# Two steps of value products in a row, six places for probabilities, and one weight loaded in each pass

## The chip, the core and the metric

The kernel is written for one NeuronCore of a Trainium2 chip. The core has five engines with queues of their own: TensorE (matrix products, its weight loads shown as PEld), VectorE (DVE), ScalarE (ACT), GpSimd (POOL) and SyncE (SP, which here only issues DMAs). They meet at semaphores alone. The metric is the device time of one execution in microseconds.

## What is computed

The reference runs a decoder of two layers over 4 sequences of 1024 rows of 256, with a context of 154 rows for each:

```python
x = x + attn0(layernorm(x))              # 16 heads of 16, causal, keys and values mixed with a gated memory
x = x + xattn0(layernorm(x), ctx, ctx)   # 16 heads, rotary, keys from the context
x = x + ffn0(layernorm(x))               # quantised linear, depthwise convolution, silu
x = x + attn1(layernorm(x))              # 16 heads of 16, every row sees every row
x = x + xattn1(layernorm(x), ctx, ctx)   # one head of 256 over the context
x = x + moe(layernorm(x))                # 16 experts, 2 chosen, and a shared one

def heads(q, k, v):                      # the part that the change is about
    w = softmax(einsum('bqd,bkd->bqk', q, k) / 4.0, axis=-1)
    return einsum('bqk,bkd->bqd', w, v)
```

## The kernel before

The program is written out by hand: every engine has its own list, and waits on semaphores whose counts a first dry build works out. One pass over the program handles one sequence, so there are four passes. In a pass there are three attentions of 16 heads: "own" (causal, 8 tiles of 128 keys), "cross" (two tiles of keys, 128 and 26) and "second" (8 tiles of keys, not causal). They are called the first, the cross and the third attention in this document, and all run through the same class `Heads`, with one order of work from `attention_plan`. All engines walk through this one list, each doing its own part of an item. Heads are handled in pairs, eight pairs to an attention.

The items of the list:
- *first* (a unit `u` of a head `h`): TensorE multiplies queries by keys into one of three banks (4, 5 and 6, taken in turn by `ring`; L646, up to 512 columns; causal units add a mask, L652 or L649). VectorE takes the maximum of each row (L796, into `tops`). These maxima are needed before the real scores. In the third attention a pair has 32 units.
- *join* and *cut*: VectorE joins the maxima (L803), and GpSimd cuts each into three bf16 parts (L846 to L849).
- *top*: TensorE turns the parts (L725, a bank of the ring), ScalarE copies them (L769), and SP writes them by DMA (L909) as three more rows under the queries of the pair.
- *score* (a step `s` of 128 keys, and one of its parts): TensorE computes the scores again, turned, with the maxima subtracted by those three rows (L674), for both heads of the pair, into one of two pairs of banks (0 and 1, 2 and 3). ScalarE takes the exponential (L756) and writes it into a place of `probs`. There are four places, used in turn. In the first attention GpSimd clears the masked half for pairs 1 to 5 (L837); for the others TensorE adds a mask (L678).
- *value*: TensorE multiplies values by the probabilities (L708) into bank 7, and sums over the steps. A product has 32 output rows and takes one of four strips of the array: heads times parity of the tile. The operands are f32, so each of the four is two instructions, eight for a step.
- *gather*, *spin* and *norm*, after the last step of a pair: ScalarE copies bank 7 (L763), TensorE turns it (L717, a bank of the ring), VectorE divides by the sum (L812, L814).
- *turn*, once per four pairs: the output is turned for the projection (L731).

`attention_plan` sets how these mix. Scores and values make the main list. A step of scores has one or two parts, and a step's values come as soon as the steps after it have two parts:

```python
            held.append((pair, s))
            while sum(len(steps[later]) for _, later in held[1:]) >= 2:
                value(*held.pop(0))
```

The first scores run ahead of that list by a lead, and are dealt out evenly between its entries (`upto`): per pair of the third attention 32 units over 24 entries. SP loads the queries and keys of pair + 3 (L863, L869) once the last scores of a pair are in. ScalarE's exponential `n` waits for the values that read the place four before it.

Weights of the last attention (`xattn1`) stay in memory for the whole program, among them `wide_q`, 128 x 512 words; it is used once per pass, near the end of the third attention (L1685).

## Time and profile before

| | us |
|---|---|
| median of three runs | 3350.33 |
| lowest and highest of them | 3348.94, 3357.76 |
| the profiled execution | 3356.7 |
| its span, from first to last instruction | 3355.1 |

The profile shows one execution. Each engine has a busy time; a matmul's record lasts longer than the time until the next can follow, so two matmuls overlap in the records, and distances between starts tell more than durations. A line of the timeline merges like instructions in a row: start, time from the first start to the last end, engine, line of the kernel, operation, what is written and read, shapes, and their count; in brackets the idle time of the engine ahead of it and what ended that. The page's last part lists DMA issues with the median time from issue to landing.

### The profile page before, as it was taken

How to read it: one execution, taken by the hardware profiler on the slowest of the kernel's cores; microseconds unless marked ns; L12 is line 12 of the kernel's file. 1: busy time of each engine (PE TensorE's matmuls, PEld its weight loads, DVE VectorE, ACT ScalarE, POOL GpSimd, SP SyncE). 2: the span in 40 equal slices, each digit the busy share in tenths (PEclk: the TensorE clock that was granted, in tenths of full speed). 3: DMA queues.
4: the chain of work that ended last, by engine and by line, in shares of the span. 5: the costliest groups of instructions: out<-in, count | busy, mean ns of one | idle time of the engine just before them, and what ended most of it. 6: DMA issues, size and time to landing. Idle time of an engine off the chain costs nothing.

```text
span 3355.1 us, 46975 instructions
## 1 busy us (share of the span) xinstructions
PE 3191.1 (95%) x17720; PEld 1713.3 (51%) x17720; DVE 2323.0 (69%) x4331; ACT 1782.8 (53%) x2551; POOL 634.7 (19%) x1166
## 2 busy tenths in 40 slices
PE   6999889999999989999999998999999999899999
PEld 4444433378644443337864444334786444433477
DVE  7856688556685578856678557885667855788555
ACT  3565546643456555664355555566424655556632
POOL 0322010024132201012403120100340321020033
PEclk9999999999999999999999999999999999999999
DMA  3212011023121202111312020120231202021023
GB/s 138 51 34 39 1 34 34 11 65 114 32 52 26 40 1 38 30 35 53 115 38 43 18 40 1 39 39 25 63 105 42 40 17 39 5 44 30 10 84 96
DMA packets 118101, 147.74 MB, mean 44 GB/s; under 512 B 25384, under 2 KB 75920, under 8 KB 117596
## 3 DMA queue, kind: packets, MB, share of 16 engines
q1 hardware_dynamic: 117876, 144.74, 18.1%
q8 instruction: 141, 2.31, 0.3%
q14 instruction: 84, 0.69, 0.1%
HBM read 74.25 MB, written 4.46 MB: 23 GB/s over the span
## 4 chain that ended last, share of the span: by engine, by line
PE 51%; DVE 8%; ACT 4%; issue 2%; DMA 1%; SPq 1%; POOL 0%; DVEq 0%; ACTq 0%
PE psum L1908 13%; PE psum L708 9%; PE psum L674 8%; PE psum L646 7%; PE psum L1000 4%; DVE small L796 3%; ACT work L756 2%; PE psum L939 1%; PE psum L717 1%; PE psum L500 1%; DMA work<-work 1%; PE psum L481 1%; PE psum L929 1%; SPq L863 1%; PE psum L1734 1%
## 5 line engine op out<-in xcount | busy, mean ns | idle before, releaser
L796 DVE TENSOR_REDUCE small<-psum 128x1 f32<-128x512 f32 (+6 forms) x1856 | 1136.7, 656 | 210.2 <-PE psum L646 175.9
L756 ACT ACTIVATE work<-psum 128x1024 f32<-128x1024 f32 (+5 forms) x1024 | 918.3, 935 | 419.4 <-PE psum L674 317.4
L646 PE MATMUL psum<-work 96*128 96x512 bf16 (+4 forms) x2688 | 655.7, 308 | 32.8 <-DVE small L796 16.2
L1908 PE MATMUL psum<-rounded_work 128*128 128x512 f32 x2592 | 602.0, 394 | 9.9 <-DVE rounded_work L1994 6.5
L674 PE MATMUL psum<-work 99*128 99x512 bf16 (+4 forms) x2048 | 564.2, 358 | 6.9 <-ACT work L756 4.0
L1908 PEld LDWEIGHTS psum<-rounded_work 128*128 128x128 f32 x2592 | 489.9, 190 | 116.0 <-DVE rounded_work L1994 8.3
L708 PE MATMUL psum<-work 128*32 128x512 f32 (+4 forms) x4480 | 532.3, 528 | 1.6 <-ACT work L756 1.4
L646 PEld LDWEIGHTS psum<-work 96*128 96x128 bf16 x2688 | 233.5, 97 | 544.4 <-DVE small L796 332.2
L674 PEld LDWEIGHTS psum<-work 99*128 99x128 bf16 (+1 forms) x2048 | 178.5, 97 | 199.3 <-ACT work L756 63.1
L2009 ACT CAST rounded_work<-work 128x512 fp32r<-128x512 f32 x144 | 89.4, 621 | 344.5 <-DVE work L2050 321.7
L846 POOL CAST small<-small 128x16 bf16<-128x16 f32 x96 | 18.8, 196 | 1156.2 <-DVE small L803 586.8
L1438 PE MATMUL psum<-ident_bf 128*128 128x512 bf16 x808 | 201.3, 380 | 8.7 <-DVE work L1539 4.5
L812 DVE RECIPROCAL small<-psum 128x16 f32<-128x16 f32 x96 | 24.7, 257 | 243.1 <-PE psum L717 243.1
L2055 DVE TENSOR_TENSOR rounded_work<-work,rounded_work 128x512 fp32r<-128x512 f32 x144 | 118.4, 822 | 107.2 <-ACT rounded_work L2009 107.2
L1885 POOL CAST rounded_work<-work 128x256 fp32r<-128x256 f32 x192 | 100.3, 523 | 435.9 <-PE psum L1908 421.8
L708 PEld LDWEIGHTS psum<-work 128*32 128x32 f32 (+1 forms) x4480 | 94.0, 107 | 171.4 <-issue 143.9
L2045 DVE TENSOR_TENSOR work<-work,psum 128x512 f32<-128x512 f32 x144 | 98.7, 685 | 99.5 <-PE psum L1908 89.4
L1886 POOL TENSOR_TENSOR rounded_work<-work,rounded_work 128x256 fp32r<-128x256 f32 x192 | 148.1, 772 | 15.4
L1438 PEld LDWEIGHTS psum<-ident_bf 128*128 128x128 bf16 x808 | 77.8, 98 | 93.1 <-DVE work L1539 7.8
L2050 DVE TENSOR_TENSOR work<-work 128x512 f32<-128x512 f32 x128 | 114.2, 892 | 14.7 <-DMA work<-combine 10.4
L1000 PE MATMUL psum<-xT,qkv 128*128 128x512 f32 x256 | 113.1, 593 | 2.7 <-ACT xT L488 2.7
L1000 PE MATMUL psum<-xT,work 128*128 128x512 f32 x256 | 110.5, 592 | 0.0
(297 smaller groups left out, 3765.2 us busy)
## 6 DMA issues: line engine op xcount, KB each, us to landing
work<-work SPq DMA_DIRECT2D x320, 192.0 KB, 4.3
work<-combine SPq DMA_DIRECT2D x64, 512.0 KB, 4.1
work<-in_w_gate SPq DMA_DIRECT2D x64, 128.0 KB, 3.5
work<-in_w_up SPq DMA_DIRECT2D x64, 128.0 KB, 3.5
work<-in_w_down SPq DMA_DIRECT2D x64, 128.0 KB, 3.8
work<-in_x SPq DMA_DIRECT2D x8, 512.0 KB, 4.9
out<-x SPq DMA_DIRECT2D x8, 512.0 KB, 2.9
work<-work SPq DMA_DIRECT2D x64, 28.9 KB, 2.0
```

Source lines behind the costliest of these rows:

```text
L646: ins = nc.tensor.matmul(dst[:, c * n:(c + 1) * n], A.q_pair[0:ROWS, slot, h, P * i:P * (i + 1)], A.k_of(pair, h)[0:ROWS, s0:s0 + n], star ...
L674: ins = nc.tensor.matmul(dst[0:size, 0:P * many].rearrange("p (i c) -> p i c", c=P), A.k_of(pair, h)[0:MORE_ROWS, P * s:P * s + size], til ...
L708: ins = nc.tensor.matmul(dst, V_head, moving, start=(s == 0), stop=(s == A.ns - 1), skip_group_check=True)
L756: nc.scalar.activation(probs[0:size, n % 4, :, 0:P * many], banks(2 * (n % 2), 2)[0:size, :, 0:P * many], ACT.Exp, scale=DH ** -0.5).then_ ...
L796: nc.vector.tensor_reduce(tops[:, pair % 2, places[0]:places[-1] + 1:step], src, AX.X, ALU.max) \
L1000: ins = nc.tensor.matmul(out, w[:, a, P * k:P * (k + 1)], xT[:, a, 1 + HALF * half:1 + HALF * (half + 1)], start=(a == 0), stop=(a == KD - 1))
L1438: nc.tensor.matmul(bank(place).rearrange("p (a c) -> p a c", c=P), ident_bf[:, :], spread(ident_bf[:, :], 1, 4), start=True, stop=True, sk ...
L1885: pool_own(nc.gpsimd.tensor_copy(shape(hi_w), source))
L1886: ins = nc.gpsimd.tensor_tensor(shape(lo_w), source, shape(hi_w.bitcast(F32)), ALU.subtract)
L1908: ins = nc.tensor.matmul(dst, a_parts[i], b_parts[j], start=start and n == 0, stop=stop and n == 2, skip_group_check=True)
L2050: nc.vector.tensor_tensor(value, value, row[e % 2][:, HALF * half:HALF * (half + 1)], ALU.mult).then_inc(*up("unit_full", u))
L2055: nc.vector.tensor_tensor(hid_low[:, u % 4, :], value, hid_high[:, u % 4, :].bitcast(F32), ALU.subtract).then_inc(*up("unit_ready", u))
```

## The change

The values of two steps are multiplied one behind the other, once the steps after the two have two parts. So the entries of the main list are fewer (20 in place of 24 per pair of the third attention), and the first scores are dealt out over them. `probs` has six places. `wide_q` leaves the weights that stay; SP loads it into the work area in each pass, behind the *top* of pair 6 of the third attention and ahead of that pair's rows, after the heads in the loaded slots have landed, and TensorE waits for it ahead of its use. In the changed file lines after the planner stand 4 to 10 lower.

```diff
+PROBS = 6
...
-    def value(pair, s):
-        pieces = [("value", pair, s)]
-        if s == len(steps) - 1:
+    def values(pair, s):
+
+        pieces = [("value", pair, s), ("value", pair, s + 1)]
+        if s + 1 == len(steps) - 1:
             pieces.append(("gather", pair))
...
             held.append((pair, s))
-            while sum(len(steps[later]) for _, later in held[1:]) >= 2:
-                value(*held.pop(0))
-    for which in held:
-        value(*which)
+            while sum(len(steps[later]) for _, later in held[2:]) >= 2:
+                values(*held[0])
+                held = held[2:]
+    for which in held[::2]:
+        values(*which)
...
-        probs = area.take(4, 2, HALF)
+        probs = area.take(PROBS, 2, HALF)
...
+        wide_q = area.take(KD, D)
...
-                    if n >= 4:
-                        act.wait_ge(*at("valued", a, *A.order[n - 4][0:2]))
+                    if n >= PROBS:
+                        act.wait_ge(*at("valued", a, *A.order[n - PROBS][0:2]))
...
                         sp.wait_ge(*at("scored", a, A.last_of(pair - A.slots, A.ns - 1)))
+                    if a == "second" and pair == PAIRS_OF_HEADS - 2:
+                        for loaded in range(PAIRS_OF_HEADS - SLOTS, PAIRS_OF_HEADS):
+                            for h in range(2):
+                                sp.wait_ge(*at(LOADED[2 * (loaded % SLOTS) + h], a, loaded))
+                        nc.sync.dma_start(wide_q, io["wide_q"]).then_inc(*up("context_keys_landed", "wide_q", by=16))
...
                 if n == 2:
+                    pe.wait_ge(*at("context_keys_landed", "wide_q"))
                     for a in range(KD):
-                        ins = project(dst[:, S * a:S * (a + 1)], lambda k: resident["wide_q"][:, k, P * a:P * (a + 1)], wide_kT)
+                        ins = project(dst[:, S * a:S * (a + 1)], lambda k: wide_q[:, k, P * a:P * (a + 1)], wide_kT)
```

Where the instructions stand, in three places. In the middle of a pair of the third attention TensorE's list before is this (L646 first scores, L674 scores, L708 values):

```order
L646 MATMUL psum<-work 128x512 x2
L674 MATMUL psum<-work 128x512 x2
L646 MATMUL psum<-work 128x512
L708 MATMUL psum<-work 32x512 x4
L646 MATMUL psum<-work 128x512
L674 MATMUL psum<-work 128x512 x2
L646 MATMUL psum<-work 128x512 x2
```

and now, with the same three as L650, L678 and L712:

```order
L650 MATMUL psum<-work 128x512 x2
L678 MATMUL psum<-work 128x512 x2
L650 MATMUL psum<-work 128x512
L678 MATMUL psum<-work 128x512 x2
L650 MATMUL psum<-work 128x512 x2
L678 MATMUL psum<-work 128x512 x2
L650 MATMUL psum<-work 128x512 x2
L678 MATMUL psum<-work 128x512 x2
L650 MATMUL psum<-work 128x512
L712 MATMUL psum<-work 32x512 x8
```

Values come once for four score pairs and eight units, not once for two and four.

At the top transpose of the third attention (L725, now L729) TensorE's list is, before, with the semaphores that each waits for:

```order
L725 MATMUL psum<-ident_bf,small 48x128 [waits largest,top_cut]
L674 MATMUL psum<-work 128x512 [waits prob]
L674 MATMUL psum<-work 128x512
L646 MATMUL psum<-work 128x512 [waits largest] x2
L674 MATMUL psum<-work 128x512 [waits prob]
L674 MATMUL psum<-work 128x512
L646 MATMUL psum<-work 128x512 [waits top_turned]
L708 MATMUL psum<-work 32x512 x4
L646 MATMUL psum<-work 128x512 [waits largest]
L674 MATMUL psum<-work 128x512 [waits prob,top_rows_landed_1]
```

and now:

```order
L729 MATMUL psum<-ident_bf,small 48x128 [waits largest,top_cut]
L650 MATMUL psum<-work 128x512 [waits largest]
L678 MATMUL psum<-work 128x512 [waits prob]
L678 MATMUL psum<-work 128x512
L650 MATMUL psum<-work 128x512 [waits largest]
L678 MATMUL psum<-work 128x512 [waits prob]
L678 MATMUL psum<-work 128x512
L650 MATMUL psum<-work 128x512 [waits top_turned]
L650 MATMUL psum<-work 128x512 [waits largest]
L678 MATMUL psum<-work 128x512 [waits prob,top_rows_landed_1]
```

The scores that wait for the landed rows still come third after the transpose, with no values ahead of them.

On SP, near the end of the third attention, the list now is (L867 and L873 load keys and queries, L918 writes the rows of a top, L917 the weight):

```order
L867 DMA work<-work 96x1x1024 x2
L873 DMA work<-work 96x1x1024 x2
L917 DMA work<-in_wide_q 128x512
L918 DMA work<-work 3x16x128 x2
```

The new transfer stands ahead of the rows of pair 6; before, those rows followed the loads of the pair before.

## Rows read from the trace of the kernel before

**Rows 1.** Busy time by stage: first and third attention of pass one (columns: stretch, length, busy and count per engine, TensorE clock, DMA)

```profile
121.70:245.20 123.50, 122.37 (x1021) 53.96 (x1020) 84.85 (x153) 79.51 (x118) 38.58 (x93) 1.00 0.20 38
482.00:665.30 183.30, 182.29 (x1041) 56.88 (x1040) 141.70 (x238) 129.08 (x142) 10.33 (x29) 1.00 0.12 23
```

**Rows 2.** Timeline of one cycle of the third attention: TensorE, VectorE, ScalarE

```profile
562.73 0.39 PE L646 MATMUL psum<-work 96*128 96x512 bf16 x1
...
562.95 0.60 PE L674 MATMUL psum<-work 99*128 99x512 bf16 x2
...
563.59 1.94 ACT L756 ACTIVATE work<-psum 128x1024 f32<-128x1024 f32 x2 [0.90 <-PE psum L674]
...
564.25 0.38 PE L646 MATMUL psum<-work 96*128 96x512 bf16 x1
564.56 0.16 PEld L708 LDWEIGHTS psum<-work 128*32 128x32 f32 x8 [0.42 <-issue]
...
565.56 0.39 PE L646 MATMUL psum<-work 96*128 96x512 bf16 x1
```

**Rows 3.** Timeline of shorter stretches in the same cycle: VectorE, and the value matmuls

```profile
563.15 0.69 DVE L796 TENSOR_REDUCE small<-psum 128x1 f32<-128x512 f32 x1 [0.30 <-PE psum L646]
564.41 1.28 DVE L796 TENSOR_REDUCE small<-psum 128x1 f32<-128x512 f32 x2
565.02 0.61 PE L708 MATMUL psum<-work 128*32 128x512 f32 x4
```

**Rows 4.** Timeline of the third attention from a top transpose to the next pair's scores

```profile
568.72 0.24 PE L725 MATMUL psum<-ident_bf,small 128*48 128x128 bf16 x1
568.83 0.69 DVE L796 TENSOR_REDUCE small<-psum 128x1 f32<-128x512 f32 x1 [0.19 <-PE psum L646]
...
569.27 0.78 SPq L909 DMA_DIRECT2D work<-work  x1
...
569.57 0.10 PEld L646 LDWEIGHTS psum<-work 96*128 96x128 bf16 x1 [0.36 <-DVE small L796]
...
571.54 0.39 PE L646 MATMUL psum<-work 96*128 96x512 bf16 x1
571.65 0.23 PEld L674 LDWEIGHTS psum<-work 99*128 99x128 bf16 x2
```

**Rows 5.** Timeline of the first attention behind the last values of a pair

```profile
167.92 0.39 PE L646 MATMUL psum<-work 96*128 96x512 bf16 x1
...
168.16 0.59 ACT L763 COPY work<-psum 128x512 f32<-128x512 f32 x1
...
168.78 1.02 ACT L756 ACTIVATE work<-psum 128x1024 f32<-128x1024 f32 x1
```

**Rows 6.** Timeline of TensorE at the end of the first attention

```profile
244.39 1.08 PE L708 MATMUL psum<-work 128*32 128x128 f32 x20
245.40 0.70 PE L929 MATMUL psum<-x,ident 128*128 128x512 f32 x1
```

**Rows 7.** The page's DMA issues: issuer, count, KB each, us to landing

```profile
work<-in_w_gate SPq DMA_DIRECT2D x64, 128.0 KB, 3.5
...
work<-in_x SPq DMA_DIRECT2D x8, 512.0 KB, 4.9
...
work<-work SPq DMA_DIRECT2D x64, 28.9 KB, 2.0
```

**Rows 8.** Timeline of the third attention: rows of a top, then a spin a pair before rows 4

```profile
545.56 0.79 SPq L909 DMA_DIRECT2D work<-work  x1
...
551.43 0.66 PE L717 MATMUL psum<-ident,work 128*128 128x128 f32 x4
...
552.90 0.10 PEld L646 LDWEIGHTS psum<-work 96*128 96x128 bf16 x1 [0.44 <-DVE xn L814]
```

**Rows 9.** Timeline of TensorE at the end of the third attention

```profile
656.02 1.04 PE L674 MATMUL psum<-work 99*128 99x512 bf16 x4
...
660.19 0.39 PE L674 MATMUL psum<-work 99*128 99x512 bf16 x1
```

More of the change, by code:

```diff
@@ L696, in heads_tensor @@
                                 i0, _, many = A.steps[s][part]
-                                moving = probs[0:size, A.number[(pair, s, part)] % 4, h, 0:P * many]
+                                moving = probs[0:size, A.number[(pair, s, part)] % PROBS, h, 0:P * many]
                                 dst = bank(7)[rows, P * (i0 // 2):P * (i0 // 2 + many)]
@@ L704, in heads_tensor @@
                                     continue
-                                moving = probs[0:size, A.number[(pair, s, 0)] % 4, h, 0:P * tiles].rearrange("p (i c) -> p i c", c=P)[:, j0::2, :]
+                                moving = probs[0:size, A.number[(pair, s, 0)] % PROBS, h, 0:P * tiles].rearrange("p (i c) -> p i c", c=P)[:, j0::2, :]
                                 k0 = (i0 + j0) // 2
@@ L834, in heads_gpsimd @@
                     n, pair, s, _ = key
[L835 removed]
+                    block = probs[:, n % PROBS, :, 0:P]
                     pool.wait_ge(*at("prob", a, n))
```

7 lines of the change are left out of this document (3 added, 4 removed).

## The prediction, as it was made before the changed kernel ran

> **What bounds the kernel now.** I read the stages first, then single cycles of the order of work, and the page's list of DMA issues for prices. The first and the third attention take 123.5 and 183.3 us of each of four passes; TensorE is busy 99% of both at a granted clock of 1.00, but in the third VectorE has 141.7 us of spans and ScalarE 129.1, so neither is far behind [rows 1].
>
> [Rows 2] is one cycle of the third attention; below, F is a matmul of first scores (L646) that VectorE reduces (L796), S a pair of score matmuls (L674) that ScalarE exponentiates (L756), and V the eight instructions that multiply values (L708). The cycle is F S F F S F V and takes 565.56 - 562.73 = 2.83 us. Nobody stops TensorE in it: F follows F every 0.22 us. These latencies are used throughout:
> - VectorE starts 0.42 us after its F (562.73 to 563.15). Queued reductions start 0.60 apart (1.28 for two, less 0.68 to 0.69 for one) [rows 2, 3], and TensorE goes on 0.05 after an end (568.83 + 0.69, then 569.57) [rows 4]. So the fourth F after F1 waits, if at all, for the start of F1's reduction + 0.75.
> - ScalarE starts 0.64 after its S (562.95 to 563.59); queued ones start 0.92 apart (1.94 - 1.02 [rows 2, 5]). A bank pair is free 1.07 after such a start.
>
> **What a joint is worth.** V begins 0.31 after the last F (564.25 to 564.56), where 0.22 is normal: 0.09 for the way in. From V to the next F are 1.00 us; its first four instructions run 0.46 ahead of the second four [rows 2, 3], so the last four take 0.54, where 512 columns twice at 2.4 GHz need 0.43: 0.11 for the way out. With the loading of the first weights (0.02 to 0.03) a joint saves about 0.23. A row checks this. The last twenty instructions of the first attention, three steps, stand in a row and take 245.40 - 244.39 = 1.01 us [rows 6]. Their columns (at most 256, 128 and 128, twice each) need 0.85; with three first loads and ways out (0.14 each) and two ways in they would take 1.45. Two joints saved 0.44. Two steps in a row then take 1.86 from their first matmul to the next F. There are 72 joints in a pass, 288 in all: 67 us if TensorE were the only limit.
>
> The trace shows eight loads of weights within 0.16 us, those of the second four among them, while the first four matmuls run until 0.46 [rows 3]; the loads of a second step can hide likewise. The Trainium skill ("TensorE: Matmul & The Clock Gate", on packing small matmuls, The mechanism) says that a load overlaps a running matmul only when its row group differs, and here all rows are the same. By that rule a joint would save the way in alone. The rows speak against it.
>
> **The third attention, walked through.** Joining V makes the rest denser: the new cycle is F F S F S F F S F F S F VV, with eight F and four S. TensorE alone would need 2 x 2.83 - 0.23 = 5.43. But F has three banks and S two pairs, and all S now come between two VV. From the first F at 0: F1 0, F2 0.23, S1 0.44, F3 0.88, S2 1.09, F4 1.52; F5 waits for the second reduction, 1.77; S3 waits for S1's exponential (0.44 + 0.64 + 1.07), 2.15; F6 2.60; the reductions started at 0.42, 1.02, 1.63 and 2.23, so F7 waits until 2.98; S4 3.21, F8 3.64, VV 3.95, next F 5.80. Against 5.67 for two old cycles the plain new cycle is **0.13 us longer**: VV is a stretch of 2.17 us in which VectorE has only three banks to empty.
>
> *The cycle with the top rows.* Before, the top transpose starts at 568.72, ScalarE copies it, the DMA is issued at 569.27, and the load for the next pair's first S begins at 571.65, 0.11 after its F instead of the usual 0.01: I take it that it waits for the rows' landing [rows 4]. So this S can start 2.93 after the transpose at the earliest (a DMA of 28.9 KB lands 2.0 after its issue [rows 7], which bounds it at 2.6 from below). Before, a V stood between the two; now none does. The transpose starts at 0.23, the S that needs the rows would come at 2.32 and must wait to 3.16. The walk then gives F6 3.61, F7 3.83, S4 4.05, F8 4.48, VV 4.79, next F 6.65. The old two cycles took 571.54 - 565.56 = 5.98 [rows 2, 4]. Loss 0.67 (at the other bound 0.3).
>
> *The cycle with the spin.* Old: a pair takes 569.27 - 545.56 = 23.71 [rows 4, 8], of which 23.71 - 5.98 - 2 x 5.67 = 6.39 are left for this cycle; the F that needs the spin's bank comes 1.47 after it (551.43 to 552.90), when the rows are normalised [rows 8]. New, by the same walk: spin 0.88, F3 1.38, F5 2.40, F7 3.61, VV 4.58, next F 6.43. Loss 0.04.
>
> A pair of heads is then 2 x 5.80 + 6.65 + 6.43 = 24.7 against 23.7. Of the 32 VV of the stage 26 lie in this regime: 13 plain (+1.7), 6 tops (+4.0), 7 spins (+0.3); one pair also has two more transposes, which fill waits (-0.4). Together +5.6 us a pass.
>
> *The end of the stage*, where no F is left: before, S S V S S V took 660.19 - 656.02 = 4.17 [rows 9]. New: S1 0, S2 0.44; exponentials start at 0.64 and 1.56; S3 1.72, S4 2.64, VV 3.17, next S 5.03. ScalarE idles during VV, since only two pairs of banks can be full. Three such cycles cost 2.6; the start and the last two steps, of which one waits for its exponential before and after, give back some 0.3: +2.3.
>
> *The weight.* SP issues 256 KB before the rows of pair 6, in each pass. Its own wait costs nothing: the heads that it names landed long before, since pair 7's first scores already ran. No row has this size: 128 KB land in 3.5 us, 512 KB in 4.9 [rows 7]; I take 4, and the rows behind it on the queue at 4.9 in place of 3.1: the S of this cycle waits **1.8 us** more (bounds 0.7, one issue by SP of that length, and 2.7). Its reader comes some twenty us later. At the start a transfer goes away that stands behind the ones the first steps wait for: 0.
>
> Third attention: 5.6 + 2.3 + 1.8 = +9.7 a pass.
>
> **The first attention.** Joints: four per pair, -0.93 of some 15.4 (123.5 / 8). Against it: after the last two steps of a pair ScalarE gathers, and now both exponentials of the next pair's step stand right ahead of that. The copy starts 0.49 after VV instead of 0.24 (167.92 to 168.16 [rows 5]); with its 0.59 and 0.05 the spin is at 1.13 (0.88 before), F4 waits for its bank until 2.60, F5 3.21, F6 3.81, VV 4.12. Without waits VV would be at 3.31, so 0.81 is waited where 0.23 was: +0.58. Left over is -0.35 a pair, -2.3 for six and a half. In its end without F, ScalarE again idles during VV, over narrower steps: of the 0.86 per cycle above I take 0.35 for three, +1.0. Sum -1.3 (bounds -4 and 0).
>
> **The cross attention.** Per pair one joint. Its transposes and spins already leave waits for banks, which may take some back or fill: I take the joint alone, 8 x 0.23 = -1.9 (bounds -3 and 0). The two more places for probabilities keep any exponential from waiting for a V; they cost nothing.
>
> **Sum.** 9.7 - 1.3 - 1.9 = +6.5 us a pass, +26 in four. The profiled execution took 3356.7 us and would take 3382.7; the median of the three runs, 3350.3, lies 6.4 below it. So **3376 us**. About 0.3%, 10 us, is what a measurement can tell from no change.
>
> **Rivals.**
> 1. *TensorE is what counts everywhere*: banks and ScalarE keep up, all joints pay. 3350 - 67 = 3283. For it: 99% busy. Against: the same latencies put no wait into the old plain cycle and put the old one after a top transpose where it is (568.83 + 0.75 = 569.58 [rows 4]), and the new order meets waits in every cycle. A milder form, with the first two attentions paying whole (160 x 0.23 = 37) and the third even: 3313. Together 0.12.
> 2. *The rows' DMA is not on the path*: the load at 571.65 was late by chance. Then the top cycle is 5.85 (-0.13), the weight costs nothing, and the third stage loses 1.7 - 0.8 + 0.3 - 0.4 + 2.3 = 3.1, which the other two return: 3350. Chance 0.15.
> 3. *A joint saves only the way in*: the second step's weights don't load under running matmuls. Each VV is 0.14 longer; in the first two stages that is 160 x 0.14 = 22, and in the third, whose waits cover some of it, half of its 128 x 0.14: 3376 + 31 = 3407. Chance 0.06.
> This last is what the Trainium skill's rule on loads, cited above, would give.
>
> **How the numbers follow.** Forecast 0.67, its own range 3358 to 3396 (bounds of the top cycle 4 x 6 x 0.37 = 9, of the weight 4, of the first attention 11, of the cross attention 8, not all one way). Rival 1 lies below, rival 3 above; rival 2 is inside if the range reaches 3345. Range 3345 to 3397. Slower by over 0.3% (above 3360): 0.67 less 0.04, plus 0.06, and a little of rival 2: 0.71. Same: 0.15 + 0.02, less a little: 0.16. Faster: 0.13.
>
> **What would show it.** In the third attention, a cycle between two VV of 5.8 us with waits of F for VectorE (0.3) and of S for ScalarE; 1.86 from VV to F; the S after a top transpose 2.9 behind it, and some 4.8 behind in pair 6; the stage near 193 us, the first near 122. Wrong would be a VV of over 1.95, a cycle of 5.45, or a top cycle below 6.

## The result, and the profile of the changed kernel

The changed kernel takes 3398.3 us (median of four, 3396.2 to 3401.7), the kernel before 3353.9 beside it (median of four). The ratio is 1.013, 95% interval 1.012 to 1.015: slower by 44 us, where +26 was forecast and 3397 was the upper end of the range. The profiled execution has a span of 3394.9 us against 3355.1.

The page's groups for first scores, scores and values come first, of before (L646, L674, L708) and then of after (L650, L678, L712). Columns: line, engine, operation, operands, count, busy us and mean ns of one, then the idle time of TensorE ahead of them and what ended most of it.

```profile
L646 PE MATMUL psum<-work 96*128 96x512 bf16 (+4 forms) x2688 | 655.7, 308 | 32.8 <-DVE small L796 16.2
L674 PE MATMUL psum<-work 99*128 99x512 bf16 (+4 forms) x2048 | 564.2, 358 | 6.9 <-ACT work L756 4.0
L708 PE MATMUL psum<-work 128*32 128x512 f32 (+4 forms) x4480 | 532.3, 528 | 1.6 <-ACT work L756 1.4
```

```profile
L650 PE MATMUL psum<-work 96*128 96x512 bf16 (+4 forms) x2688 | 647.8, 309 | 39.4 <-DVE small L800 21.1
L678 PE MATMUL psum<-work 99*128 99x512 bf16 (+4 forms) x2048 | 564.8, 358 | 46.4 <-ACT work L760 23.5
L712 PE MATMUL psum<-work 128*32 128x512 f32 (+4 forms) x4480 | 479.9, 524 | 2.5 <-ACT work L760 2.4
```

The same 4480 instructions for values are busy 52 us less: the joints do what they should. The idle time ahead of scores grows from 6.9 to 46.4 us. That is most of what changed sides, but not all: loads that wait lie under running matmuls, and their price is seen only in distances.

So I measure each attention from its first score pair (S) to the first product behind it (L929, now L938). The busy time in two of these stretches of pass one, the first and the third attention, answers to [rows 1]; before first, then after (columns as there):

```profile
118.32:245.40 127.08, 125.60 (x1039) 55.16 (x1038) 87.45 (x158) 82.14 (x120) 41.80 (x96) 1.00 0.20 37
...
478.69:665.79 187.10, 185.84 (x1055) 57.87 (x1054) 145.01 (x244) 131.76 (x144) 10.33 (x29) 1.00 0.12 22
```

```profile
120.91:247.71 126.80, 121.51 (x1039) 58.59 (x1038) 84.88 (x158) 81.22 (x120) 41.52 (x96) 1.00 0.20 37
...
481.87:679.76 197.89, 187.09 (x1055) 60.73 (x1054) 140.02 (x244) 131.00 (x144) 10.31 (x29) 0.99 0.12 22
```

In the first attention TensorE is busy 4.1 us less and the stage is 0.3 us shorter: nearly all of it turned into waiting. In the third it is busy no less and waits eleven us (197.89 - 187.09) instead of one. As means of the four passes, beside the forecast:

| us a pass | before | after | change | forecast |
|---|---|---|---|---|
| first attention | 127.11 | 126.83 | -0.3 | -1.3 |
| cross attention | 49.09 | 51.43 | +2.3 | -1.9 |
| third attention | 187.11 | 196.61 | +9.5 | +9.7 |
| sum | | | +11.6 | +6.5 |

Four passes of 11.6 are 46 us; the spans differ by 39.8, since stretches outside the attentions happened to be some 6 us shorter in this execution, and the medians by 44.4. Apart from the third attention a stage repeats from pass to pass, and in the same order from kernel to kernel, within 0.2 us (only the cross attention's last pass is 0.3 longer in the joined order), so single profiles of variants can be compared stage by stage.

**A plain cycle of the third attention**, timeline of TensorE and its loads (start, us, engine, line, operation, operands, count; answers to [rows 2, 3]):

```profile
542.75 1.93 PE L712 MATMUL psum<-work 128*32 128x512 f32 x16
...
543.21 0.13 PEld L712 LDWEIGHTS psum<-work 128*32 128x32 f32 x4 [0.30 <-issue]
543.64 0.13 PEld L712 LDWEIGHTS psum<-work 128*32 128x32 f32 x4 [0.30 <-issue]
...
544.61 0.60 PE L650 MATMUL psum<-work 96*128 96x512 bf16 x2
...
545.05 0.60 PE L678 MATMUL psum<-work 99*128 99x512 bf16 x2
...
546.38 0.10 PEld L650 LDWEIGHTS psum<-work 96*128 96x128 bf16 x1 [0.36 <-DVE small L800]
546.76 0.11 PEld L678 LDWEIGHTS psum<-work 99*128 99x128 bf16 x2 [0.28 <-ACT work L760]
546.77 0.61 PE L678 MATMUL psum<-work 99*128 99x512 bf16 x2
```

The double step takes 544.61 - 542.75 = 1.86 us, exactly as forecast, and the weights of its later instructions load while earlier ones run (543.21, 543.64). Then, against the forecast's clock with the first F at 0: S1 at 0.44 (forecast 0.44), the fifth F waits for VectorE at 1.77 (1.77), S3 for ScalarE until 2.16 (2.15). Cycles between two double steps take 5.80 and, where the join of the maxima falls into them, 5.87.

**The cycle with the top transpose** (answers to [rows 4]):

```profile
550.49 0.39 PE L650 MATMUL psum<-work 96*128 96x512 bf16 x1
...
550.81 0.24 PE L729 MATMUL psum<-ident_bf,small 128*48 128x128 bf16 x1
...
553.64 0.60 PE L678 MATMUL psum<-work 99*128 99x512 bf16 x2 [0.72 <-DMA work<-work]
...
557.12 0.39 PE L650 MATMUL psum<-work 96*128 96x512 bf16 x1
```

The pair's first score starts 2.83 behind the transpose and TensorE stands still for it; the cycle takes 557.12 - 550.49 = 6.63, forecast 6.65. All such waits of pass one, by the view of waits of TensorE in that stage (who waits for whom, us in total, times, longest):

```profile
PE psum L678 <- DMA work<-work: 5.3, 6, 1.5
PE psum L650 <- DVE small L800: 1.0, 6, 0.2
```

**The cross attention**, which the forecast took without a walk. The timeline of VectorE, GpSimd and TensorE in the middle of a pair:

```profile
321.99 0.20 DVE L807 TENSOR_REDUCE small<-small 128x16 f32<-128x48 f32 x1
...
322.31 0.20 POOL L850 CAST small<-small 128x16 bf16<-128x16 f32 x1 [5.96 <-issue]
...
323.15 0.22 POOL L853 TENSOR_TENSOR small<-small 128x16 bf16<-128x16 f32 x1
...
323.42 0.24 PE L729 MATMUL psum<-ident_bf,small 128*48 128x128 bf16 x1 [0.56 <-POOL small L853]
```

From the join (321.99) the cut's four instructions take until 323.37, and the top transpose waits 0.56 us with nothing running. It is now reached sooner behind the join (1.43 us here, waiting included), since the values that stood between the two have moved behind it; before, it started 1.90 behind the join and waited for nobody. A pair takes 7.01 us (top transpose to top transpose), where it took 6.49.

### The profile page after: what moved, and what is told of

The parts are those of the page before. It is cut to its first block and busy times, and to the rows that moved or that the text cites. A ratio compares the mean times of both kernels' runs of the same rounds, so it can differ in the third digit from the quotient of the medians.

```text
span 3394.9 us, 46874 instructions
## 1 busy us (share of the span) xinstructions
PE 3171.6 (93%) x17720; PEld 1734.1 (51%) x17720; DVE 2290.9 (67%) x4331; ACT 1781.6 (52%) x2551; POOL 634.9 (19%) x1166
## 5 line engine op out<-in xcount | busy, mean ns | idle before, releaser
L800 DVE TENSOR_REDUCE small<-psum 128x1 f32<-128x512 f32 (+6 forms) x1856 | 1108.4, 654 | 277.9 <-PE psum L650 264.2
L650 PE MATMUL psum<-work 96*128 96x512 bf16 (+4 forms) x2688 | 647.8, 309 | 39.4 <-DVE small L800 21.1
L678 PE MATMUL psum<-work 99*128 99x512 bf16 (+4 forms) x2048 | 564.8, 358 | 46.4 <-ACT work L760 23.5
L712 PE MATMUL psum<-work 128*32 128x512 f32 (+4 forms) x4480 | 479.9, 524 | 2.5 <-ACT work L760 2.4
L650 PEld LDWEIGHTS psum<-work 96*128 96x128 bf16 x2688 | 230.0, 97 | 484.3 <-DVE small L800 294.0
L678 PEld LDWEIGHTS psum<-work 99*128 99x128 bf16 (+1 forms) x2048 | 173.3, 97 | 234.4 <-ACT work L760 88.2
L712 PEld LDWEIGHTS psum<-work 128*32 128x32 f32 (+1 forms) x4480 | 117.8, 109 | 216.2 <-issue 188.0
## 6 DMA issues: line engine op xcount, KB each, us to landing
work<-work SPq DMA_DIRECT2D x64, 28.9 KB, 2.0
```

The costliest lines, as they stand in the source:

```text
L650: ins = nc.tensor.matmul(dst[:, c * n:(c + 1) * n], A.q_pair[0:ROWS, slot, h, P * i:P * (i + 1)], A.k_of(pair, h)[0:ROWS, s0:s0 + n], star ...
L678: ins = nc.tensor.matmul(dst[0:size, 0:P * many].rearrange("p (i c) -> p i c", c=P), A.k_of(pair, h)[0:MORE_ROWS, P * s:P * s + size], til ...
L712: ins = nc.tensor.matmul(dst, V_head, moving, start=(s == 0), stop=(s == A.ns - 1), skip_group_check=True)
L800: nc.vector.tensor_reduce(tops[:, pair % 2, places[0]:places[-1] + 1:step], src, AX.X, ALU.max) \
```

## The experiments

Stage lengths of the kernels, as above (means of four passes, from their profiles; the whole is the median where there are several runs, and for the kernels from rows_unread to spin_later_single it is one run), with the lead-in of the third attention (its first first score to its first score) where it matters:

| kernel | first | cross | third | whole, us |
|---|---|---|---|---|
| before | 127.11 | 49.09 | 187.11 | 3353.9 |
| after | 126.83 | 51.43 | 196.61 | 3398.3 |
| none_joined | 127.12 | 49.09 | 188.01 | 3354.4 |
| first_joined | 126.84 | 49.10 | 187.98 | 3354.4 |
| cross_joined | 127.12 | 51.44 | 187.69 | 3365.4 |
| third_joined | 127.10 | 49.08 | 198.56 | 3392.4 |
| rows_unread | 126.76 | 51.43 | 191.06 | 3376.3 |
| rows_unread_single | 127.11 | 49.09 | 186.79 | 3354.7 |
| weight_behind | 126.82 | 51.43 | 195.47 | 3395.8 |
| lead_14 (lead-in 28.1, not 25.6) | 126.81 | 51.43 | 194.63 | 3396.6 |
| lead_14_top_7 (lead-in 27.5) | 126.78 | 51.44 | 192.89 | 3391.7 |
| half_reduced (lead-in 21.2) | 126.80 | 51.45 | 193.47 | 3365.1 |
| tail_single | 126.04 | 51.43 | 194.91 | 3386.9 |
| dealt_by_steps | 129.90 | 48.74 | 201.16 | 3422.0 |
| cross_late_top | 126.81 | 49.36 | 197.52 | 3395.6 |
| own_spin_later | 123.39 | 51.43 | 197.62 | 3388.1 |
| spin_later_single | 125.17 | 48.46 | 185.02 | 3335.8 |
| spin_later_timed | 125.15 | 48.46 | 185.01 | 3333.7 |
| own_joined_spin_later | 122.47 | 48.46 | 185.01 | 3325.2 |
| two_joined_spin_later | 122.53 | 47.81 | 185.01 | 3321.5 |

The kernel before ran between 3346.8 and 3359.6 us in 23 runs, so a whole time of one run says little, and these variants are judged by their stages. The third attention of a joined kernel varies by one or two us in the mean and up to 4 from pass to pass (tail_single 193.8 to 197.8), with the landing of its rows at pair 6 and with a fall of TensorE's clock behind it, shown below; differences below that are read from single pairs.

### Which attention loses

One edit to the changed kernel says which attentions are joined; the places and the moved weight stay. In none_joined it is none, in the others one.

```diff
-def attention_plan(keys, causal, lead, extra, beside):
+def attention_plan(keys, causal, lead, extra, beside, group=2):
...
-        pieces = [("value", pair, s), ("value", pair, s + 1)]
+        pieces = [("value", pair, s + k) for k in range(group)]
...
-                self.units, self.steps, self.plan = attention_plan(keys, causal, lead, list(extra), beside)
+                self.units, self.steps, self.plan = attention_plan(keys, causal, lead, list(extra), beside, 2 if tag in JOINED else 1)
```

none_joined: 

> The changed kernel with the values of every step by themselves again, so the kernel before with six places and the weight loaded in each pass. Theory: only the weight's transfer counts, 0.7 to 0.8 us a pass at the first scores of pair 6: +3 us, about 3357, the three attentions as long as before. If the two more places cost anything it shows in the stages (over 183.5 us from first to last values in the third). Rival: the weight's transfer costs more elsewhere, +7 us and over.

first_joined: 

> Joined in the first attention only. Theory: a pair 15.65 us in place of 15.88, given back at the start and the end: -0.3 us a pass, with the weight about 3356. If each joint paid whole (32 x 0.23 = 7.4 a pass) 3327.

cross_joined: 

> Joined in the cross attention only. Theory from the new trace: the top transpose waits for GpSimd's cut there, a pair takes 7.0 us in place of 6.5, the attention 51.4 in place of 49.1: +2.3 us a pass and 3 for the weight in all: about 3366. The forecast's -1.9 a pass would give 3349.

third_joined: 

> Values of two steps joined in the third attention only. Theory: that attention, from its first scores to its end, 196.2 us as in the changed kernel (187.1 before), the other two as before; +9 us a pass, +36 in all: about 3390. If the loss were shared, less than +25.

Measured against 3354.7 (three rounds): none_joined ratio 1.000 (0.999 to 1.001), first_joined 1.000 (0.999 to 1.001), cross_joined 1.004 (1.003 to 1.005), third_joined 1.011 (1.009 to 1.014). Against none_joined the parts are 0, +11 and +38 us, 49 in all; the three in one kernel give +44. The profiled execution of third_joined, the slowest of its four (3402.2), has a third attention 2 us longer than the changed kernel's, by the fall of the clock shown below. So the parts add up within the intervals, the loss is real in two of the three attentions, and the third's is the one that was forecast. The places for probabilities cost nothing: the first and the cross attention of none_joined are as before. The stage table shows the weight by itself: 188.0 in place of 187.1.

### The third attention: rows, banks, end, weight

rows_unread and rows_unread_single take the landing of the rows out of the changed kernel and out of the kernel before. Left out are the three rows in the scores of the third attention; they are still made and written.

```diff
-                    if (s, part) == (0, 0):
+                    if (s, part) == (3 if a == "second" else 0, 0):
                         pe.wait_ge(*at(ROWS_LANDED[slot], a, pair))
+                    depth = ROWS if a == "second" else MORE_ROWS
```

> The changed kernel; in the third attention the scores leave out the three rows with the maxima, so that the first score of a pair needn't wait for their landing (the rows are still made and written; the fourth step waits for them). Theory: the rows' landing sets the cycle with the top transpose (6.65), which falls to about 6.0, and the weight's 0.8 us a pass goes too: third attention 196.6 -> 191.9, the whole 3379. Rival (the cycle is set by the banks of VectorE and ScalarE): only the weight's share goes, 195.8, the whole 3395.

> The kernel before, with the same left out: scores of the third attention without the rows of the maxima. By both theories the rows are hardly waited for in the old order (0.10 us in each of seven tops): third attention 187.1 -> 186.5, the whole 3352. If it falls by over 2 us, the old order waited for the rows as well and the comparison of the two orders has to be made without them.

Measured: 191.06 (theory 191.9, rival 195.8) and 186.79 (186.5). The rows cost the joined order 5.5 us a pass, the weight's share among them, and the single one 0.3. The cycle with the transpose falls to 5.95, while the plain ones stay at 5.79 and 5.87, so it isn't the three rows less in each score that help. Without the rows the joined stage is still 4.3 us longer than the single one. The joined timeline at the same place, first the transpose, then the load for the score that no longer waits for a DMA but for ScalarE, 2.10 behind it:

```profile
547.52 0.24 PE L730 MATMUL psum<-ident_bf,small 128*48 128x128 bf16 x1
...
549.62 0.11 PEld L679 LDWEIGHTS psum<-work 96*128 96x128 bf16 x2 [0.49 <-ACT work L761]
```

It also settles how [rows 4] was to be read. In rows_unread_single the load for that score starts 0.01 behind its first score's, as usual:

```profile
572.24 0.39 PE L646 MATMUL psum<-work 96*128 96x512 bf16 x1
572.25 0.32 PEld L675 LDWEIGHTS psum<-work 96*128 96x128 bf16 x2
```

In the kernel before it started 0.11 behind. So it had waited for the landing, 2.93 behind the transpose. Its matmul starts 3.05 behind the transpose in both, so it lost next to nothing by that (0.05 us a pair).

half_reduced makes the reductions of the third attention shorter by leaving out the right half of each tile:

```diff
-                    nc.vector.tensor_reduce(tops[...], src, AX.X, ALU.max) \
+                    nc.vector.tensor_reduce(tops[...], src[:, :, 0:n // 2] if a == "second" else src, AX.X, ALU.max) \
```

> The changed kernel; in the third attention VectorE takes the maximum over the left half of each tile of first scores only, so its reductions are shorter (0.3 to 0.4 us instead of 0.60); the other half is left out. Theory: in the plain cycle of 5.80 us first scores wait 0.2 us for VectorE's three banks and scores 0.16 for ScalarE; with short reductions only ScalarE's waits stay, the cycle takes 5.68, the third attention about 194 in place of 196.3. Rival (the double step itself, or ScalarE, makes the cycle long): 5.80 stays, and the stage with it.

The plain cycles take 5.68 each (534.29 to 539.97 here), as forecast, and only scores wait in them:

```profile
534.29 1.92 PE L712 MATMUL psum<-work 128*32 128x512 f32 x16
...
538.29 0.11 PEld L678 LDWEIGHTS psum<-work 99*128 99x128 bf16 x2 [0.52 <-ACT work L760]
...
539.21 0.11 PEld L678 LDWEIGHTS psum<-work 99*128 99x128 bf16 x2 [0.37 <-ACT work L760]
...
539.97 0.64 PE L712 MATMUL psum<-work 128*32 128x512 f32 x4
```

So VectorE's three banks are what the plain cycle has above 5.68, and ScalarE's two pairs hold it there, above the 5.43 that TensorE alone would need. The cycle with the spin falls from 6.42 to 5.98, which the expectation didn't name; the one with the transpose stays at 6.64, held by the rows. The stage falls by 3.1 us in all. It would be more, but behind the weight the double step is slow in all four passes here (2.26 to 3.18 us, by the clock shown below).

lead_14 and lead_14_top_7 look for a place where the joined order escapes its waits. The first lets the first scores of the third attention run 14 ahead instead of 10, the second also puts its top transpose behind the seventh unit of the next pair:

```diff
-                                    Heads("second", FULL, False, 10, q_pair, slot_keys, V, ...
+                                    Heads("second", FULL, False, 14, q_pair, slot_keys, V, ...
```

```diff
-                if pair and 2 * u + h == min(TOP_LAG, per_pair - 1):
+                if pair and 2 * u + h == min(top_lag, per_pair - 1):     # 7 in the third attention, else 4
```

> The changed kernel, with the first scores of the third attention 14 ahead of the main list instead of 10, so that a top transpose comes 2.5 entries (about 3 us) earlier against the score that reads its rows. Theory: the rows' landing was on the path and no longer is, as in the run without reading them (191.1 us from the first score to the end of the third attention, where 196.6 were); four units less in the mix give 190.2. The start, where first scores stand alone at 0.60 us each, grows by 2.4. Sum -3.9 us a pass, the whole 3382. Rival (leaving out the rows helped because scores read 96 partitions instead of 99, or for another reason than their landing): the stage stays at 195 or over, the start still costs 2.4, the whole 3405.

> The changed kernel, third attention with a lead of 14 as before, and its top transpose behind the seventh unit of the next pair instead of the fourth, so that it stands right ahead of a double step of values. The run with the lead alone kept a cycle of 6.70 us with the transpose: the rows were in time, but the transpose waited 0.89 us for GpSimd's cut. Theory (the joined order has no place between a cut that comes too late and rows that come too late, unless both numbers are moved): the cycle falls to 5.95, the third attention from 194.1 to 188.9, the whole to 3376. Rival (a dense cycle takes one more bank of the ring only at this price): the cycle stays at 6.5 or over, the stage at 193.

Both missed. With the lead no score of a middle pair waits for a row, but the stage is 194.1 in three passes, not 190.2, and the cycle with the transpose takes 6.64 to 6.71. The transpose moved into the dense end of a cycle, close behind the join, and there TensorE stands still:

```profile
523.35 0.22 POOL L853 TENSOR_TENSOR small<-small 128x16 bf16<-128x16 f32 x1
523.62 0.10 PEld L729 LDWEIGHTS psum<-ident_bf,small 128*48 128x48 bf16 x1 [1.19 <-POOL small L853]
523.62 0.24 PE L729 MATMUL psum<-ident_bf,small 128*48 128x128 bf16 x1 [0.89 <-DVE small L800]
```

The profile names VectorE for the matmul's wait and GpSimd for its load's; the cut ended last. With the transpose three units later the cut is in time, the cycle takes 6.37, and what is left is the bank that the transpose takes from the ring and the join on VectorE:

```profile
524.30 0.22 PE L729 MATMUL psum<-ident_bf,small 128*48 128x128 bf16 x1 [0.24 <-DVE small L800]
```

192.2 us in two of the four passes (193.1 and 194.2 in the others) lie between theory (188.9) and rival (193), nearer the rival. Part of the gain goes to the lead-in, 2.0 us longer than in the changed kernel. No order tried here brings a joined third attention below the single one's 187.1.

tail_single takes the values of the last pair of each attention one step at a time:

```diff
+    def many(held):
+        return group if held[0][0] < PAIRS_OF_HEADS - 1 else 1
```

> The changed kernel, with the values of the last pair of each attention taken one step at a time, where no or few first scores are left. Theory: without first scores a double step leaves ScalarE idle; the end of the third attention (30.93 us behind the last first score, 27.68 in the kernel before) returns to 28.4, those of the first and cross attentions by 0.3 and 0.2; sum -3.0 us a pass, the whole 3386. Rival (the end is longer because more work is pushed behind the last first score): the third attention's end returns by less than 1 us, the whole 3395.

The end of the third attention (from the last first score) takes 28.56 us (28.4 expected), where the changed kernel takes 30.93 and the kernel before 27.68. In the cross attention nothing changes (0.2 expected), in the first 0.8 instead of 0.3. What the joined end looks like, TensorE's timeline of the changed kernel (answers to [rows 9]):

```profile
669.24 1.92 PE L712 MATMUL psum<-work 128*32 128x512 f32 x16
...
672.82 0.60 PE L678 MATMUL psum<-work 99*128 99x512 bf16 x2 [0.68 <-ACT work L760]
673.74 0.61 PE L678 MATMUL psum<-work 99*128 99x512 bf16 x2 [0.31 <-ACT work L760]
674.27 1.92 PE L712 MATMUL psum<-work 128*32 128x512 f32 x16
```

674.27 - 669.24 = 5.03, the number of the forecast, against 4.17 for two single cycles.

weight_behind issues the weight behind the rows of pair 6. Its diff moves the block with `wide_q`'s DMA three lines down, below the DMA of the rows.

> The changed kernel, with the DMA of the weight issued behind the rows of pair 6 instead of ahead of them. Theory: the weight costs only what it delays these rows, and the score that reads them stood 3.66 us behind its top where the other pairs have 2.84 to 2.93; it returns to at most 2.95, the stage falls by 0.8 us a pass, the whole by 3 to 3395. The prediction's own term was 1.8 us a pass; if that was right and another loss hid in the 3.66, the stage falls by 1.8. Rival (the weight costs where its reader waits): the score comes back, but the projection that reads the weight waits instead, the whole stays at 3398.

The score comes 2.86 to 2.95 behind the transpose of pair 6 in all passes (3.66, 3.58, 3.45 and 3.58 in the changed kernel), and the stage is 1.1 us shorter in the mean: more than the 0.8 expected. The rest is in pass one, and there it isn't a wait. The changed kernel around that score, TensorE and SyncE:

```profile
626.62 0.36 SPq L917 DMA_DIRECT2D work<-in_wide_q  x1
...
627.05 0.79 SPq L918 DMA_DIRECT2D work<-work  x1
```

```profile
629.73 0.60 PE L678 MATMUL psum<-work 99*128 99x512 bf16 x2 [1.55 <-DMA work<-work]
...
631.65 3.25 PE L712 MATMUL psum<-work 128*32 128x512 f32 x16
634.84 0.60 PE L650 MATMUL psum<-work 96*128 96x512 bf16 x2
```

The double step at 631.65 takes 3.19 us instead of 1.86. Its granted clock says why (columns as in [rows 1], the clock is third from the end):

```profile
629.70:631.65 1.95, 1.92 (x7) 0.60 (x7) 1.06 (x2) 1.28 (x2) 0.00 (x0) 0.83 0.00 0
631.65:634.83 3.18, 3.18 (x17) 0.59 (x16) 0.82 (x2) 0.71 (x1) 0.00 (x0) 0.57 0.00 0
634.83:636.50 1.67, 1.67 (x14) 1.03 (x11) 1.24 (x3) 1.17 (x2) 0.00 (x0) 1.00 0.00 0
```

TensorE had stood still for 1.55 us, and then ran for some 3 us mostly at its lower level, 1.2 GHz: 1.3 us more. In third_joined the same double step takes 3.25 to 3.58 us in all four passes, in weight_behind never.

### The cross attention: the cut

cross_late_top puts its top transpose one unit later:

```diff
-                if pair and 2 * u + h == min(TOP_LAG, per_pair - 1):
+                if pair and 2 * u + h == min(top_lag, per_pair - 1):     # 5 in the cross attention, else 4
```

> The changed kernel, with the top transpose of the cross attention one unit later (behind the fifth unit of the next pair, not the fourth). Theory: the cross attention lost its joint to the cut of GpSimd, for which the top transpose waited 0.56 us with TensorE empty; now a pair of score matmuls and one unit stand in that time, a pair takes 6.45 us in place of 7.01, the stage 48 in place of 51.4, the whole 3385. Rival (ScalarE's gather and exponentials set the pair): the wait only moves to the next score, the stage stays within 0.5 of 51.4, the whole 3398.

A pair takes 6.38 us (6.45 expected), and the transpose, which now stands right ahead of the double step, waits for nobody:

```profile
307.74 0.22 POOL L853 TENSOR_TENSOR small<-small 128x16 bf16<-128x16 f32 x1
...
308.13 0.22 PE L729 MATMUL psum<-ident_bf,small 128*48 128x128 bf16 x1
308.27 2.06 PE L712 MATMUL psum<-work 128*32 128x512 f32 x16
```

The stage falls by 2.1 us of the 3.4 expected. In pass one the three cycles between double steps in its middle are 0.57 to 0.63 shorter and the fourth 0.46; the later ones, where no first scores are left, are as long as in the changed kernel, and the first double step comes 0.3 later, since the score ahead of it now waits 0.43 for its rows. The mechanism is shown for the pairs in the middle: this wait was their loss, and without it a pair is 0.11 us shorter than with single steps (6.38 against 6.49). The stage stays 0.3 above the 49.1 of single steps, at its start and its end.

dealt_by_steps deals first scores out thinner, in all three attentions:

```diff
-    per_main = len([x for x in main if x and x[0][0] in ("score", "value")]) / PAIRS_OF_HEADS
+    weight = lambda x: 0 if not x or x[0][0] not in ("score", "value") else 2 if x[0][0] == "value" else 1
+    per_main = sum(weight(x) for x in main) / PAIRS_OF_HEADS
...
-        upto = min(len(firsts), int(per_pair + lead + k * per_pair / per_main))
+        upto = min(len(firsts), int(per_pair + lead + passed * per_pair / per_main))
+        passed += weight(entry)
```

> The changed kernel, with a double step of values counted as two entries when the first scores are dealt out, so that they lie as thin between scores as before (1.33 per entry of the third attention, not 1.6) and more of them stand behind the values. Theory (what the joint gives is lost where first scores stand close together, to their banks, to the cut and to the rows): in the cross attention the top transpose now has the values behind it and one more score ahead, its wait of 0.56 us goes and a pair takes about 6.4 us in place of 7.0 (stage 51.4 -> 48); in the third attention the order is F F (F) S F S F S FF S FF V V, a walk with the latencies of the trace gives 5.9 for the plain cycle where 5.80 was, because the first scores of a cycle now come first and scores wait for ScalarE: stage 196.6 -> 199. First attention about 1 us less. Sum about -2 us a pass, 3390. Rival (the banks of VectorE are what limits everywhere, and thinner dealing helps everywhere): third attention 196.6 -> 193, sum -7 a pass, 3370.

The cross attention takes 48.7 (48 expected), below the single order. The third takes 201.2 (199 expected by the theory, 193 by the rival), so thin dealing doesn't help where all banks are short. The first attention takes 3.1 us more where I expected 1 less; this I did not follow up.

### The first attention: the spin

own_spin_later turns the gathered values of the first attention one entry later:

```diff
-            after(2, "spin", pair)
-            after(2, "norm", pair)
+            after(spin, "spin", pair)     # 3 in the first attention, else 2
+            after(spin, "norm", pair)
```

> The changed kernel, with the spin and the norm of the first attention one entry later. Theory: in the first attention the joints' gain goes in the 0.30 us that the spin waits for ScalarE's gather, and in the 0.49, 0.27 and 0.27 that first scores wait for its bank and for VectorE behind it; later the gather is done, a pair takes 15.1 us in place of 15.65, the stage (from first score to end) 123.5 in place of 126.8, the whole 3385. Rival (the waits would come at another place, since VectorE and ScalarE are short of time): the stage stays over 126.

The changed kernel behind the last values of a pair, TensorE and its loads (answers to [rows 5]):

```profile
155.67 0.66 PE L721 MATMUL psum<-ident,work 128*128 128x128 f32 x4 [0.30 <-ACT work L767]
...
157.13 0.10 PEld L650 LDWEIGHTS psum<-work 96*128 96x128 bf16 x1 [0.49 <-DVE xn L818]
...
157.73 0.10 PEld L650 LDWEIGHTS psum<-work 96*128 96x128 bf16 x1 [0.27 <-DVE small L800]
```

and the kernel with the later spin (its lines stand one lower):

```profile
154.86 0.60 PE L722 MATMUL psum<-ident,work 128*128 128x128 f32 x4
155.30 0.60 PE L651 MATMUL psum<-work 96*128 96x512 bf16 x2
```

A pair takes 15.07 (15.1 expected) instead of 15.65, the stage 123.4 (123.5 expected). Whose gain is that? spin_later_single makes the same edit to the kernel before, in all three attentions.

> The kernel before, with spin and norm one entry later in all three attentions. It says whose gain the 3.4 us a pass of the same move in the changed kernel are. Theory: with single steps the spin hardly waits for the gather, the first attention falls from 127.1 to 125.6 at most, so that in the joined order the move gave back what the joint had lost. Rival (the gain is that of the later spin in any order): the first attention falls to 123.7. In the third attention the cycle with the spin (3.56 us) may fall to 3.3, the stage from 187.1 to 185.3.

The first attention falls to 125.2 (125.6 by the theory, 123.7 by the rival): not by 3.4 as in the joined order, but by 2.0. The other 1.5 us a pass are what the joints had lost to the spin. The third attention falls to 185.0 (185.3 expected), since its cycle with the spin takes 3.28 in place of 3.56, and the cross attention by 0.6.

### Put together

own_joined_spin_later joins the first attention alone, single in its last pair, with the later spin everywhere and the weight behind the rows; two_joined_spin_later also joins the cross attention, dealt by steps there. spin_later_timed is the kernel before with the later spin, timed beside them.

> The changed kernel with double steps in the first attention only (single ones in its last pair), spin and norm one entry later in all three attentions, and the weight behind the rows. By the stages of the earlier runs: first attention 123.4 less 0.8 = 122.6 us a pass (kernel before 127.1, single steps with the later spin 125.15), cross 48.46, third 185.0; sum -7.2 us a pass, so 3355 - 29 = 3326. Theory: a joint is worth its 0.23 us only where nobody waits behind it. Rival (the weight's move costs elsewhere, or the parts don't add up): 3335 or over, no better than the later spin alone.

> The same with double steps in the cross attention too, there dealt by steps (a double one counts as two entries), so that its top transpose no longer waits for the cut. Theory: eight joints of 0.23 less waits: the cross attention takes 47.5 in place of 48.46, the whole 3322. Rival (in the cross attention the joints stay without gain, since GpSimd and ScalarE set the pair): 48.4 or over, the whole 3326 or over.

> The kernel before with the later spin alone, timed beside the two. By the stages of its first run: -4.7 us a pass, 3336; the joints of the first attention are then worth the difference to the first kernel, 2.5 us a pass or 10 in all.

Measured: 3325.2 (ratio 0.991, 0.990 to 0.993), 3321.5 (0.990, 0.989 to 0.992) and 3333.7 (0.994, 0.993 to 0.995), against 3354.1 for the kernel before. All three are within 2.5 us of what the stages gave. Against the later spin alone, joints in the first attention return 2.7 us a pass and in the cross attention 0.65. They number 28 and 7 (in the first attention the last pair is single; in the cross attention it ended on two steps in a row before, too), so a joint yields about 0.1 us of its 0.23 once the waits at the spin and the cut are gone. In the first attention of pass one TensorE is busy 4.1 us less than with the later spin alone (120.39 against 124.48) and idle 1.4 us more (2.02 against 0.66); which waits take the rest I didn't split.

## Why the prediction was right in direction and short in size

- **A joint's worth, 0.23 us, and 1.86 for two steps**: right; 1.86 in every double step of full width.
- **Third attention, +9.7**: right in sum (+9.5), and in its walk. Plain cycle 5.80 (5.80), in pass one cycle with the transpose 6.63 to 6.73 (6.65), with the spin 6.42 (6.43), a pair 24.7 to 24.8 (24.7), score behind the transpose 2.82 to 2.94 (2.93). The walk from three latencies of the old trace was enough. That the rows' landing sets the cycle with the transpose, and not the banks, is shown by rows_unread; that VectorE sets the plain one down to 5.68, by half_reduced. Rivals 1 and 2 fall with them. That the sum is within 0.2 is luck in part: the next two terms are off by 0.95 and 0.7, in opposite directions.
- **The end, +2.3**: measured +3.25. The three cycles of 5.03 were right (0.86 each, 2.6). The -0.3 for the start and the last two steps should have been about +0.65; which of them costs it wasn't looked at.
- **The weight, +1.8**: mis-sized; 1.1 in the changed kernel by weight_behind. The score stands 3.5 to 3.7 behind its transpose, not 4.8: the rows behind the weight on the queue were late by one issue and a little more, near the lower bound of 0.7, and my 4.9 for their landing had taken them to wait for the whole transfer. In pass one the fall of the clock came on top.
- **First attention, -1.3**: measured -0.3. The gain per pair was put too large and counted too often: a pair takes 15.65 against 15.88, -0.23 where -0.35 was forecast, and the five distances between top transposes that are shorter add up to -1.2, not -2.3. The end costs 0.9 (the last distance 16.08 against 15.29, and 0.1 behind it), forecast 1.0.
- **Cross attention, -1.9**: this is the step that failed, with +2.3. "Its transposes and spins already leave waits for banks, which may take some back or fill: I take the joint alone" put a bound of 0 on a stage that I hadn't walked. The change moved the top transpose against the join, as in the third attention, and here GpSimd's cut was not in time: 0.56 us per pair, more than twice the joint. The run cross_late_top, where this wait is gone, shows that it isn't the whole of the 4.2 us between forecast and measurement: it returns 2.1, and a pair then gains 0.11, not 0.23. The rows that would have told it, the join, the four GpSimd instructions and the transpose, are in any trace of the kernel before.
- **72 joints in a pass**: this counts double steps. The order before already had values of two steps in a row five times in a pass, three of them in the first attention (two in the twenty instructions of [rows 6]), one each in the others; the changed order has 73 such places, so 68 are new. Rival 1's 67 us and the eight joints of the cross attention (seven) are a little too high for that.

The errors of the first and the cross attention are 1.0 and 4.2 us a pass, 21 in four, and account for the distance between 3376 and 3398. Rival 3 (a load doesn't hide under the values running) would have given 3407, near the measured time, for a wrong reason: a double step of 1.86 us leaves no room for it. The rule of the Trainium skill ("TensorE: Matmul & The Clock Gate", on packing small matmuls, The mechanism) that a load overlaps a running matmul only when its row group differs does not hold for these loads of 32 columns; the rows at 542.75 to 543.64 above show 16 matmuls on the same 128 rows in 1.86 us, with loads under them.

## What to carry to other kernels

Saving switches between kinds of work on a busy engine also packs what stands between them: ask of each queue that hands over inside that stretch (banks, a short chain on a slow engine, a DMA) whether its latency still fits, and walk every stage, the short ones too, since the one not walked had the wrong sign. A transfer that was just in time costs nothing until the order gets denser; reading it away in both orders prices it at once. Before joining anything, look for handovers that already wait in the loose order: moving the spin by one entry was worth 20 us, the joints on top of it 8 to 12.

## What the runs showed of the hardware that I had not expected

- After a wait of 1.55 us TensorE's granted clock was 0.57 for 3.2 us (1.2 GHz for most of it), and a double step took 3.19 us in place of 1.86. In the other three passes the score came 0.1 to 0.2 us sooner behind its transpose, and the double step took its usual time. A stall for a DMA can cost nearly its own length again. The length of the stall alone doesn't decide it: in third_joined stalls of 1.58 to 2.05 us at this place were followed by a fall in all four passes, in tail_single stalls of 1.52, 1.57 and 1.68 us were not. What else does stays open.
- The landing of 28.9 KB of rows varies by 0.1 us from pair to pair, and behind a transfer of 256 KB by 0.6 (3.73 to 4.37 behind the transpose in none_joined, its own order giving 3.05). With the rows unread the third attention repeats within 0.01 us in all four passes, so this landing, with the fall of the clock behind it, is nearly all of the joined kernel's own scatter there.
- The load of weights waits visibly (0.11 us) while its matmul isn't late at all: an idle time of PEld is no price by itself.
